# Attention with a quantized feed-forward product: two tile pairs per half added by accumulating DMA, turned maxima beside the sums, the product in one burst, the absolute maximum by halves

## The reference

```python
Q, K, V = (proj(Wq), proj(Wk), proj(Wv))           # 512x512 weights, 16 heads of 32
att = jnp.einsum('bhqd,bhkd->bhqk', Q, K) * (1.0 / math.sqrt(Dh)) + b[0]
att = jax.nn.softmax(att * m + (1.0 - m) * NEG_INF, axis=-1)
y = jnp.einsum('bhqk,bhkd->bhqd', att, V)           # back to (512 channels, 1024 tokens)
scale = jnp.maximum(jnp.max(jnp.abs(y), axis=-1, keepdims=True), 1e-7) / 127.0
q = jnp.clip(jnp.round(y / scale), -128, 127)       # the row is a channel: its maximum is over all 1024 tokens
out = x + (q @ weight.T * scale * w_scale + bias).astype(float16)
```

## Time and profile before

| | |
|---|---|
| median of three runs | 2563.82 us (2562.51 to 2564.39) |
| profiled execution: time, span | 2565.66 us, 2563.9 us |
| PE, DVE, ACT, POOL busy | 96%, 56%, 56%, 72% |
| granted TensorE clock, mean | 0.991 of full speed |
| DMA, mean over the span | 110 GB/s |

### The profile page before, as it was taken

How to read it: one execution, slowest core, us unless ns; L and a number is a source line. 1 busy time by engine, 2 the same in 40 slices (tenths; PEclk the granted TensorE clock), 3 DMA queues, 4 the chain that set the end, 5 groups by cost and what they waited for, 6 DMA issues and landing times.

```text
span 2563.9 us, 40963 instructions
## 1 busy us (share of the span) xinstructions
PE 2455.4 (96%) x12880; PEld 1354.0 (53%) x12880; DVE 1448.3 (56%) x1459; ACT 1435.3 (56%) x2664; POOL 1853.0 (72%) x614
## 2 busy tenths in 40 slices
PE   8999999979999999999999999999999999999996
PEld 7888888864444444444444444444444444444442
DVE  3211111156666666667666666666666666666660
ACT  3222222216656666666666666666666666666664
POOL 3332222227878888888888888888888888888885
PEclk9999999989999999999999999999999999999998
DMA  6655545633333333433333333333333343433311
GB/s 246 255 194 196 196 188 188 207 133 84 89 81 92 89 85 88 95 84 84 84 95 85 84 84 84 84 84 84 84 84 93 92 95 92 90 93 85 86 41 34
DMA packets 151511, 282.62 MB, mean 110 GB/s; under 512 B 30489, under 2 KB 66329, under 8 KB 151393
## 3 DMA queue, kind: packets, MB, share of 16 engines
q10 hardware_dynamic: 49312, 130.80, 22.8%
q1 hardware_dynamic: 102080, 150.57, 16.8%
HBM read 178.29 MB, written 101.45 MB: 109 GB/s over the span
## 4 chain that ended last, share of the span: by engine, by line
PE 58%; DVE 8%; issue 7%; POOL 2%; ACT 2%; DMA 1%; DVEq 0%; ACTq 0%; POOLq 0%; SPq 0%
PE score L703 17%; PE ring L122 16%; PE pv L730 15%; DVE neg_max L131 7%; PE ring L762 4%; PE ring L740 4%; PE ring L743 2%; DVE absmax L911 1%; POOL acc L967 1%; ACT probs L807 1%; POOL y L974 0%; DMA sums<-recips_by_head 0%; DMA recips<-sums 0%; DVE scale L914 0%; POOL k_stack L116 0%
## 5 line engine op out<-in xcount | busy, mean ns | idle before, releaser
L131 DVE TENSOR_REDUCE neg_max<-ring 128x1 f32<-128x1024 f32 x1024 | 1219.0, 1220 | 572.6 <-PE ring L122 570.0
L807 ACT ACTIVATE probs<-score 128x512 f32<-128x512 f32 x2048 | 1104.0, 603 | 378.3 <-PE score L703 357.9
L967 POOL TENSOR_TENSOR acc<-acc,probs 128x2048 f32<-128x2048 f32 x254 | 1163.7, 4582 | 17.4 <-ACT probs L807 0.2
L703 PE MATMUL score<-q_stack,k_stack 100*128 100x512 f32 x2048 | 882.5, 433 | 27.9 <-ACT probs L807 15.2
L122 PE MATMUL ring<-k_stack,q_stack 98*128 98x512 f32 x2048 | 825.1, 403 | 46.3 <-DVE neg_max L131 41.9
L703 PEld LDWEIGHTS score<-q_stack,k_stack 100*128 100x128 f32 x2048 | 387.7, 190 | 489.8 <-ACT probs L807 349.1
L730 PE MATMUL pv<-probs,v_in 128*32 128x512 f32 x4096 | 546.3, 605 | 0.0
L122 PEld LDWEIGHTS ring<-k_stack,q_stack 98*128 98x128 f32 x2048 | 390.6, 191 | 150.3 <-DVE neg_max L131 90.7
L967 POOL TENSOR_TENSOR acc<-probs 128x2048 f32<-128x2048 f32 x64 | 292.6, 4572 | 150.1 <-ACT probs L807 150.1
L474 POOL TENSOR_TENSOR q_stack<-x_raw,k_stack 128x1024 fp32r<-128x1024 f32 x28 | 67.7, 2450 | 293.5 <-ACT k_stack L359 293.5
L730 PEld LDWEIGHTS pv<-probs,v_in 128*32 128x32 f32 x4096 | 80.6, 108 | 185.9 <-issue 106.3
(11 more groups left out here) (90 smaller groups left out, 1888.7 us busy)
## 6 DMA issues: line engine op xcount, KB each, us to landing
k_stack<-qk_part ACTq DMA_DIRECT2D x93, 512.0 KB
q_stack<-qk_part ACTq DMA_DIRECT2D x183, 256.0 KB, 3.9
qk_part<-part_hi SPq DMA_DIRECT2D x64, 512.0 KB, 2.6
qk_part<-part_lo SPq DMA_DIRECT2D x64, 512.0 KB, 3.5
v_steps<-v_out SPq DMA_DIRECT2D x64, 256.0 KB, 2.2
sums<-recips_by_head SPq DMA_DIRECT2D x64, 256.0 KB
res<-x ACTq DMA_DIRECT2D x32, 512.0 KB, 4.5
out<-res SPq DMA_DIRECT2D x64, 256.0 KB, 4.7
```

The costliest lines, as they stand in the source:

```text
L131: nc.vector.tensor_reduce(neg_max[:, pair // CHUNK, pair % CHUNK:pair % CHUNK + 1], ring[:, :], AX_X, ALU.max, negate=True).then_inc(neg_m ...
L703: pe.matmul(score[score_bank(t)][:, :], k_stack[par][0:ROWS, h, kt * P:(kt + 1) * P], q_stack[par][0:ROWS, half, h, :], start=True, stop=T ...
L807: nc.scalar.activation(probs[:, kt, h, :], score[score_bank(t)][:, :], ACT.Exp).then_inc(exp_done, 1)
L967: nc.gpsimd.tensor_tensor(acc[:, half, :, :], first, probs[:, k, :, :], ALU.add).then_inc(acc_done, 1)
```

## The change

The softmax sums: tile 0 is added to tile 1 and tile 2 to tile 3, in place in `probs`, by a DMA that adds (`begin_pair`), issued from GpSimd once both tiles have been multiplied by V. GpSimd then makes four additions instead of five (tile 4 plus pair 1, pair 3, tile 5, tile 6), and TensorE adds only tile 7 and `acc`. The extras are four in place of seven: each turned chunk of maxima shares the buffer and the place of a sum (units 23 and 55), the integers are turned at 51, and both halves of the product run as one burst at 59. The absolute maximum is taken by halves, after the reductions of units 27 and 39; the reciprocal of the second half's sums moves from unit 17 to 31, and ScalarE's rounding to units 41 to 44. The last half of the last step has no pairs.

```diff
-POOLED = (6, 6)
+PAIRED = 2
+FIRST, ADDED = 4, (1, 3, 5, 6)
-SUMS_1, TURN_1, TURN_Q, FFN_0, FFN_1, SUMS_0, TURN_0 = 11, 23, 41, 45, 49, 51, 55
+SUMS_1, TURN_Q, SUMS_0, FFN = 23, 51, 55, 59
...
             def turn_max(s, chunk, buf):
-                pe.transpose(buf[0:CHUNK, 0:P], neg_max[:, chunk, :], ident[:, :]).then_inc(maxT_done, 1)
+                pe.transpose(buf[0:CHUNK, N:N + P], neg_max[:, chunk, :], ident[:, :]).then_inc(maxT_done, 1)
...
+            def ffn(s, buf):
+
+                pe.wait_ge(qT_out, 2 * s + 2)
+                for half in range(2):
+                    cols = slice(half * N, (half + 1) * N)
+                    for tt in range(TT):
+                        mm = pe.matmul(buf[:, cols], qT[:, tt, :], fw[:, tt, cols], start=(tt == 0), stop=(tt == TT - 1))
+                    mm.then_inc(ffn_done, 1)
...
                     use = ("extra", t)
+                    if t == SUMS_1 and (prev or main):
+                        buf = take_ring(s, par, use)
+                        if main:
+                            turn_max(s, 1, buf)
+                        if prev:
+                            sum_rows(s - 1, 1, buf)
...
-                if prev and t == 14:
+                if prev and t == 30:
                     load_res(s - 1)
...
-                    if t in (31, 32) and prev:
-                        round_rows(s - 1, t - 31)
...
+                    if t in (41, 42) and prev:
+                        round_rows(s - 1, t - 41)
+                    if t in (43, 44) and prev:
+                        make_ints(s - 1, t - 43)
+                    if t in (52, 53) and prev:
+                        take_qT(s - 1, t - 52, ring_of(par, ("extra", TURN_Q)))
...
+            def begin_pair(s, half, i):
+
+                pool.wait_ge(pv_done, QH * TT * s + half * TT + 2 * i + 2)
+                pool.sem_inc(pair_begun, 1)
+                pool.dma_start(probs[:, 2 * i + 1, :, :], probs[:, 2 * i, :, :], accum_op=ALU.add).then_inc(pair_done[i], 16)
```

More of the change, by code:

```diff
@@ L50 @@
 RING = 8
-POOLED = (6, 6)
+PAIRED = 2
+FIRST, ADDED = 4, (1, 3, 5, 6)
+ADDS = len(ADDED)
+FREED = {FIRST: 1, **{tile: k + 1 for k, tile in enumerate(ADDED)}}
 LAST_POOLED = 4
@@ L515, in attend @@
         qT = sb("qT", [P, TT, P], BF16)
-        absmax = sb("absmax", [P, 1], F32)
+        absmax = sb("absmax", [P, 2], F32)
+        floor = sb("floor", [P, 1], F32)
         scale = sb("scale", [P, 1], F32)
@@ L561, in attend, with halves_before @@
         acc_done = sem("acc_done")
+        pair_begun = sem("pair_begun")
+        pair_done = [sem(f"pair_done{i}") for i in range(PAIRED)]
         half_done = sem("half_done")
         res_done = sem("res_done")
-        ADDS = (POOLED[0] - 1, POOLED[1] - 1)
         MAX_ROWS = 16 * 2
-        def adds_before(s, half):
-            return sum(ADDS) * s + half * ADDS[0]
+        def halves_before(s, half):
+            return QH * s + half
         def ring_of(par, use):
@@ L736, in sum_rows @@
                 last = isinstance(s, int) and (s, half) == (STEPS - 1, 1)
-                pooled = LAST_POOLED if last else POOLED[half]
-                for tile in range(pooled, TT):
+                first, adds = (LAST_POOLED, LAST_POOLED - 1) if last else (max(ADDED) + 1, ADDS)
+                for tile in range(first, TT):
                     for h in range(GH):
-                        pe.matmul(buf[h * DH:(h + 1) * DH, 0:N], ones[:, :], probs[:, tile, h, :], start=(tile == pooled), stop=False)
-                pe.wait_ge(acc_done, adds_before(s, half) + pooled - 1)
+                        pe.matmul(buf[h * DH:(h + 1) * DH, 0:N], ones[:, :], probs[:, tile, h, :], start=(tile == first), stop=False)
+                pe.wait_ge(acc_done, ADDS * halves_before(s, half) + adds)
                 for h in range(GH):
@@ L985, in step @@
             def step(s, par, prev=True, main=True, ahead=True):
+                if prev:
+                    normalise(s - 1, 0)
                 if main:
-                    for k in range(1, 4):
+                    for i in range(PAIRED):
+                        begin_pair(s, 0, i)
+                    for k in range(3):
                         add(s, 0, k)
                 if prev:
-                    for half in range(2):
-                        normalise(s - 1, half)
+                    normalise(s - 1, 1)
                 if main:
-                    for k in range(4, POOLED[0]):
-                        add(s, 0, k)
-                    for k in (1, 2):
+                    add(s, 0, 3)
+                if main and ahead:
+                    for i in range(PAIRED):
+                        begin_pair(s, 1, i)
+                    for k in range(2):
                         add(s, 1, k)
+                if main and not ahead:
+                    for k in range(1, LAST_POOLED):
+                        add_last(k)
                 if prev:
@@ L999, in step @@
                         finish(s - 1, half)
-                if main:
-                    for k in range(3, POOLED[1] if ahead else LAST_POOLED):
+                if main and ahead:
+                    for k in range(2, ADDS):
                         add(s, 1, k)
```

143 lines of the change are left out of this document (76 added, 67 removed).

## The result

The changed kernel takes 2732.63 us (median of four runs, 2725.92 to 2736.25), the kernel before 2563.16 in the same session: a ratio of 1.0661, 95% interval 1.0637 to 1.0685. It is 169 us slower. The prediction was 2574 with a range of 2505 to 2665: the direction is right, the size far off.

What follows compares the result with a forecast made beforehand. TensorE, busy 96%, was taken as the bound at 60.8 us per step. Savings of 3.66 met costs of 3.1 and 0.56; late pairs added 0.5 per step (+15), one-time savings took 6.6: 2574 us, range 2505 to 2665.

Steps and rivals of the forecast that it cites:

- sum groups and turned maxima: TensorE's sums: 8 of 24 products leave, 0.86 us saved per half; maxima turned beside the sums save 0.62 per step.
- The wait for `qT`: Unit 54's ring product waits for ScalarE's copies of the turned integers, 1.43 us late; 0.56 more per step than before.
- What it costs at unit 39: The maximum's second half waits for y; TensorE stalls and ScalarE runs late, unit 47's score 3.1 us late.
- The chain of 8.07 us: Reciprocal's start to absolute maximum's start, read at the kernel's end; against 5.92 us available, VectorE waits 2.15.
- The clock was a rival: The stall at unit 44 lowers TensorE's clock in every step: 2.8 us each, +84, 2650 us; chance 0.10.
- The stall I forecast myself: TensorE stalls 1.6 us at unit 44 for a ring buffer, behind VectorE's wait for y.
- my own case's +15 and -6.6: 30 steps times 0.5 us for the late second pair, less one-time savings of 6 and 0.6; chance 0.45.
- The forecast -6 for the second step: The second step's 1.92 us wait for turned maxima, and the half-clock stretch with it, should go: -6 us once.
- The forecast of 5.5 us per MB: Adding DMAs' pace, between 3.9 and 7.8; the first half's second pair lands at 25 us, 0.5 late.
- pairs late: Rival: at 7.8 us per MB for the adding DMAs, y is 4 us late, 2679 us; chance 0.20.
- No change through hidden costs: Rival: the pairs' lateness is hidden altogether, giving 2559 to 2563 us; chance of a time within 5 us 0.14.
- the forecast of -3.66 per step: Savings per step: products 1.72, turned maxima 0.62, one burst 0.34, absolute maximum by halves 0.98 us.

Runs made afterwards that it cites:

- e8: The changed kernel without adding DMAs, res loaded at unit 14, reciprocal at 29, maximum's second half at 43; 2561.98 us, ratio 1.0005.
- e1: The changed kernel with the load of res issued at unit 14 again instead of 30; 2712.11 us, ratio 1.0577.
- e3: The changed kernel without adding DMAs: GpSimd adds five tiles, TensorE sums tiles 6 and 7; 2744.38 us, ratio 1.0698.
- e12: The kernel before, with the absolute maximum taken two more times per step into a tile nobody reads; 2702.43 us, ratio 1.0541.
- e11: The kernel before, with the absolute maximum taken one more time per step into a tile nobody reads; 2625.3 us, ratio 1.0234.
- e4: The kernel before with the pairs alone, other units as before, GpSimd's order fitted to them; 2921.54 us, ratio 1.1391.
- e13: e6 with all of qT copied by one VectorE instruction behind the reduction of unit 51, replacing ScalarE's two copies; 2576.0 us, ratio 1.006.
- e16: e13 with the reciprocals at units 31 and 61, two later each; 2679.94 us, ratio 1.0455.
- e14: e8 with all of qT copied by one VectorE instruction behind the reduction of unit 51; 2515.44 us, ratio 0.982.
- e6: The changed kernel with res loaded at unit 14, reciprocal at 29, maximum's second half at 43, ScalarE's four operations at 45 to 48; 2565.05 us, ratio 1.0018.
- e10: The changed kernel without adding DMAs, res loaded at unit 14, maximum's second half at 43, reciprocal left at 31; 2635.88 us, ratio 1.0286.

## Why the prediction went wrong

**What held.** Most of the step's own sum. The sum groups and turned maxima fell by 0.87 per half (forecast 0.86 and 0.31). The products' part came whole, and of the 0.31 only 0.03 came, as e8 shows. The burst fell to 3.37 (3.2), and the 0.98 of the absolute maximum went. The wait for `qT` cost 1.22 us for a forecast 1.43, and its group 1.91 over the plain one for 1.98. And the mechanism: the second half of the maximum waits for `y`, TensorE for the reduction behind it.

**The step that failed** is "What it costs at unit 39", 3.1 us. The two groups took 9.44 (1541.18 - 1531.74) and 3.93 us, 7.25 over two plain ones; on average over 25 steps it is 7.27. Two terms of it were wrong:

- The chain of 8.07 us was read at the end of the kernel, "where nothing competes", and used as if nothing would compete in a step either. It took 11.42. The load of `res`, which I had noted as moved "out of the way" of the pairs, was moved onto the chain, and the pairs and the queries' loads lie near it too: without the load of `res` beside it 1.8 us of the 3.35 are gone (e1), without the pairs 2.3 (e3). The two overlap, so the shares of each aren't shown.
- The clock was a rival with a chance of 0.10 and a price of 2.8 us per step. It happens in every step, and e12 shows that a stall of 3 us is enough. The row had shown it: the clock fell near 720.9, 1 us behind the end of that idle time of 1.92 us, and TensorE then stood still once more, 1.96 us. The stall I forecast myself was 1.6 us; e11, run later, has 1.8 us and the lower clock in 16 of 26 steps, so a chance near even would have been right. (The rival's time has a slip too: with my own case's +15 and -6.6, +84 gives 2658, not 2650.)

Set against the span (+167 us): TensorE's idle time grew by 124 us, of which 77 are waits for reductions, 35 for copies of `qT` and 9 for exponentials; its busy time grew by 43, as 95 of lower clock less 52 of products. So the stall and the clock are together (77 and 95) about as large as the whole loss, and the rest nearly cancels, as was forecast.

**Once.** The forecast -6 for the second step was lost too. Its wait for the turned maxima did go, but a new one of 2.61 us stands in the first step (at 597.83), the stalls for reductions begin, and the granted clock is at its lower level 41 us between 560 and 800, where before it was 24.

**The pairs.** The additions waited for them 84 times, 1.7 us on average, where the text expected "little or not at all". The forecast of 5.5 us per MB was about right, even so, for the two pairs of a half together:
```profile
1508.68 0.84 POOL L980 DMA_DIRECT2D probs<-probs  x1
...
1515.75 4.57 POOL L996 TENSOR_TENSOR acc<-probs 128x2048 f32<-128x2048 f32 x1 [2.11 <-DMA probs<-probs]
...
1521.23 9.27 POOL L996 TENSOR_TENSOR acc<-acc,probs 128x2048 f32<-128x2048 f32 x2 [0.90 <-DMA probs<-probs]
```
The addition that needs the second pair starts 12.5 us after the first pair's issue, where the forecast had 13 (from 12 to 25). One pair takes 6.9 us from issue to landing at the median, up to 8.7 in kernels whose traffic is denser. The Trainium skill, "Collectives: The Full Stack", Part 3, has the adding transfer of a collective at half a copy's rate. By the Trainium skill's "DMA: Bandwidth & Descriptors" (Anatomy of one DMA), a copy of 1 MB is an estimated 4.4 us, of which 2.4 go by the rate; at half the rate the estimate is 6.8. The trace agrees for one pair (6.9), but no run here has a plain copy of the same tile to compare. The 7.8 us per MB of the rival "pairs late" did not come. The price was looked for in the wrong place. In the changed kernel their lateness costs nothing through `y`: the additions of the half were done at 1530.5 and the spread came at 1533.9. Their cost is what they do to other transfers (e3, e4, e13, e16), 60 us between e13 and e14, and the prediction had no term for it.

**No change through hidden costs** was near the truth only for e6 and e8, once the chain had its distance. What the forecast of -3.66 per step then still paid was the copy of `qT`, 45 us as e14 shows, the crowding of ScalarE, 0.8 us in the group of its four operations, the 0.6 of turned maxima that never came, and in e6 the 1.3 of the gather.

## What to carry to other kernels

A chain measured where nothing else runs is a lower bound (here 8.1 us, and 11.4 in a step): before a consumer is set at that distance, list every transfer that will be in flight beside it, those that the same change moves among them. Price a TensorE stall of 2 to 3 us with the lower clock, as often as it occurs: in e11 and e12 the clock doubled it. And a bulk DMA that relieves an engine is paid by the small DMAs beside it, so count who waits for those before counting what the engine saves.

## What was unexpected in the hardware

- An 8 KB gather took some 16 us from issue to use beside 1 MB pairs and a 512 KB load (e4); the 8 KB stores of the maxima landed in 1.8 us without pairs and 5.2 to 5.6 with them, those of the reciprocals in 1.4 either way (e14, e13).
- TensorE's clock, by the stall that stands once in each step between 800 and 2500 us: one of 1.2 us did not bring the lower level (e6: after none of 28; e8: after one of 27), one of 1.8 us in 16 of 26 (e11), one of 2.3 us on average in 18 of 27 (e10) and in 26 of 26 (e3, where it goes up to 3.5), one of 2.9 us in 25 of 25 (e12). In e11, stalls of the same 1.84 us went both ways.
- GpSimd is busy 0.86 us with the issue of one adding DMA.
- VectorE copies 128x1024 bf16 out of a ring buffer in 0.69 us, ScalarE 128x512 in 0.59.
